# Own keys laid down twice, and one matmul over 120 rows for their high and low values, in a cross attention and mixture of experts kernel

## What is computed

```python
x = x + xattn(layernorm(x), ctx, Wq, Wk, Wv, Wo)   # x: 32 x 56 x 512, ctx: 32 x 1500 x 512
x = x + ffn(layernorm(x), W_gate, b_gate, W_e, b_e)

def xattn(latents, context, Wq, Wk, Wv, Wo):       # 16 heads of 96, 4 key heads
    hidden = concatenate([context, latents], axis=1)        # 1500 + 56 rows
    q, k, v = latents @ Wq.T, hidden @ Wk.T, hidden @ Wv.T
    attn = softmax(einsum('bkgqd,bksd->bkgqs', q, k) * 96 ** -0.5)
    return einsum('bkgqs,bksd->bkgqd', attn, v) ... @ Wo.T

def ffn(x, W_gate, b_gate, W_e, b_e):              # 8 experts, the best 2 of each row
    top_idx = top_k(x @ W_gate + b_gate, 2)
    y = relu(x @ W_e[e] + b_e[e]) for the two experts
    return mean of the two
```

## Time and profile before

| | |
|---|---|
| time, median of 3 runs | 3424.66 us (3420.46 to 3425.6) |
| time of the profiled execution | 3425.12 us |
| its span in the profile | 3423.4 us |
| mean granted TensorE clock | 0.985 |
| PE busy | 3324.6 us, 97% of the span, 21514 matmuls |
| PEld busy | 3095.0 us, 90% |
| DVE busy | 2038.8 us, 60% |
| ACT busy | 1645.3 us, 48% |
| POOL busy | 1025.0 us, 30% |

### The profile page before, as it was taken

How to read it: one execution, slowest core, us unless ns; L and a number is a source line. 1 busy time by engine, 2 the same in 40 slices (tenths; PEclk the granted TensorE clock), 3 DMA queues, 4 the chain that set the end, 5 groups by cost and what they waited for, 6 DMA issues and landing times. The chain is left out here.

```text
span 3423.4 us, 64146 instructions
## 1 busy us (share of the span) xinstructions
PE 3324.6 (97%) x21514; PEld 3095.0 (90%) x21514; DVE 2038.8 (60%) x3003; ACT 1645.3 (48%) x3145; POOL 1025.0 (30%) x838
## 2 busy tenths in 40 slices
PE   8999999999999999999999999999999999989785
PEld 8989999999999999999999999999999999988674
DVE  5346666666666666666666666666666666665444
ACT  3225555555555555555555555555555555542231
POOL 0042222333323333333333222222222233345252
PEclk9999999999999999999999999999999999999887
DMA  6542222222222212222222222222222222217466
GB/s 222 200 142 62 59 60 64 64 64 64 60 62 62 56 51 61 58 60 63 64 63 64 64 64 64 64 60 63 59 58 63 64 64 64 65 56 209 110 197 209
DMA packets 308535, 284.53 MB, mean 83 GB/s; under 512 B 200826, under 2 KB 257650, under 8 KB 308489
## 3 DMA queue, kind: packets, MB, share of 16 engines
q1 hardware_dynamic: 301961, 265.56, 26.8%
q0 software_dynamic: 6528, 18.39, 1.6%
HBM read 208.31 MB, written 75.54 MB: 83 GB/s over the span
## 5 line engine op out<-in xcount | busy, mean ns | idle before, releaser
L815 PE MATMUL ps_proj<-wv_hi,parts 128*125 128x384 f32 x3072 | 875.6, 339 | 0.0
L760 DVE TENSOR_TENSOR probs_lo<-probs,probs_hi 125x448 fp32r<-125x448 f32 (+1 forms) x896 | 680.6, 776 | 275.7 <-ACT probs_hi L687 263.3
L802 PE MATMUL ps_proj<-parts,wk_hi 128*128 128x500 f32 x2304 | 709.8, 389 | 2.9 <-DVEq L715 2.9
L815 PEld LDWEIGHTS ps_proj<-wv_hi,parts 128*125 128x125 f32 x3072 | 559.9, 185 | 5.8
L143 POOL TENSOR_SCALAR parts<-raw 128x1000 fp32r<-128x1000 f32 (+1 forms) x198 | 239.5, 1210 | 958.1 <-PE ps_proj L815 776.7
L679 ACT ACTIVATE probs<-ps_scores 125x448 f32<-125x448 f32 (+1 forms) x896 | 462.9, 517 | 121.2 <-PE ps_scores L863 78.3
L815 PE MATMUL ps_proj<-wv_lo,parts 128*125 128x384 f32 x1536 | 518.4, 338 | 0.0
L802 PEld LDWEIGHTS ps_proj<-parts,wk_hi 128*128 128x128 f32 x2304 | 430.6, 188 | 91.0 <-DVEq L715 3.2
L687 ACT CAST probs_hi<-probs 125x448 fp32r<-125x448 f32 (+1 forms) x896 | 484.1, 540 | 28.3
L666 ACT CAST values_hi<-ps_proj 125x384 fp32r<-125x384 f32 x384 | 184.4, 480 | 645.4 <-PE ps_proj L815 645.4
L729 DVE TENSOR_TENSOR values_lo<-ps_proj,values_hi 125x384 fp32r<-125x384 f32 x384 | 214.1, 558 | 431.8 <-ACT values_hi L666 429.1
(11 more groups left out here) (199 smaller groups left out, 5720.9 us busy)
## 6 DMA issues: line engine op xcount, KB each, us to landing
raw<-in_ctx SPq DMA_DIRECT2D x192, 500.0 KB, 3.6
qk_hi<-proj_out_hi SPq DMA_DIRECT2D x60, 224.0 KB, 2.0
qk_lo<-proj_out_lo SPq DMA_DIRECT2D x60, 224.0 KB, 2.3
queries_hi<-qk_hi SPq DMA_DIRECT2D x32, 336.0 KB, 3.5
queries_lo<-qk_lo SPq DMA_DIRECT2D x32, 336.0 KB, 3.6
att_raw<-attended SPq DMA_DIRECT2D x128, 84.0 KB
probs<-att_raw SPq DMA_DIRECT2D x31, 336.0 KB, 5.8
probs<-inverse_sums SPq DMA_DIRECT2D x31, 336.0 KB, 3.1
```

Of the source, the lines that this page charges most:

```text
L760: dve.tensor_tensor(prs[1][0:R, u % PRING, 0:N], pr[0:R, u % PRING, 0:N], f(prs[0][0:R, u % PRING, 0:N]), ALU.subtract).then_inc(p_lo, 1)
L802: mm = pe.matmul(pproj[n % 2][:, 0:CS], w["wk"][a][:, j // 3, i * P:(i + 1) * P], ct[v][:, c, j // 3, :], start=(j == 0), stop=(j == 3 * K ...
L815: mm = pe.matmul(pproj[n % 2][0:VT, 0:KD], ct[a][:, t // VTC, j // 3, s], w["wv"][v][:, j // 3, :], start=(j == 0), stop=(j == 3 * KT - 1))
```

## The change

The own keys are laid down twice in the key tiles, at column S and again at column S + 64 (`PAIR`); the eight columns between are zero. The tail's scores are made for 120 columns (`TAIL`) in place of 56, so that rows 0 to 55 and rows 64 to 119 of the scores, the exponentials and the probabilities are the same. The tail's value tile holds the high values in rows 0 to 55 and the low values in rows 64 to 119, with the column of ones only beside the high ones. So the first weighing matmul of the tail gives high and low values with the high probabilities in one, and line 882's matmul is left out for the tail; the third now also adds the low values with the low probabilities. The low values' tile for the own rows is gone, with its fill; two fills of the eight columns are new.

The diff, cut to its core:

```diff
+PAIR = 64
+TAIL = PAIR + Q
...
-        kt = [sb("keys_hi", [HD, KV, SL], F32R), sb("keys_lo", [HD + HALVES, KV, SL], F32R)]
+        kt = [sb("keys_hi", [HD, KV, S + TAIL], F32R), sb("keys_lo", [HD + HALVES, KV, S + TAIL], F32R)]
...
-        vt_lo = sb("values_lo", [VT, NVT + 1, KV, HD], F32R)
+        vt_lo = sb("values_lo", [VT, NVT, KV, HD], F32R)
...
                         rows = k_d[i][b]
-                        sp.dma_start(f(kt[i][0:HD, 0:KTILES, S:SL]),
-                                     rows[:, 0:HD].rearrange("i r q -> r i q")).then_inc(qk_loaded, 16)
-                        for j in range(KTILES):
-                            sp.dma_start(f(kt[i][j * PIECE:(j + 1) * PIECE, KTILES, S:SL]),
-                                         rows[j, HD:P]).then_inc(qk_loaded, 16)
+                        for s in (S, S + PAIR):
+                            sp.dma_start(f(kt[i][0:HD, 0:KTILES, s:s + Q]),
+                                         rows[:, 0:HD].rearrange("i r q -> r i q")).then_inc(qk_loaded, 16)
+                            for j in range(KTILES):
+                                sp.dma_start(f(kt[i][j * PIECE:(j + 1) * PIECE, KTILES, s:s + Q]),
+                                             rows[j, HD:P]).then_inc(qk_loaded, 16)
 
                 def load_v(b):
-                    for i, dst in enumerate((vt_hi[0:Q, NVT, :, 0:HD], vt_lo[0:Q, NVT])):
+                    for i, dst in enumerate((vt_hi[0:Q, NVT, :, 0:HD], vt_hi[PAIR:TAIL, NVT, :, 0:HD])):
...
-                sp.wait_ge(consts, 3)
+                sp.wait_ge(consts, 4)
...
-                for n, ap in enumerate((f(vt_hi[:, NVT]), f(vt_lo[:, NVT]), mrow[:], ident[:], own[:])):
+                for n, ap in enumerate((f(vt_hi[:, NVT]), f(kt[0][:, :, SL:S + PAIR]), mrow[:], ident[:], own[:])):
...
-                for n, (ap, value) in enumerate(((kt[1][HD:HD + HALVES], -1.0), (vt_hi[:, 0:NVT, :, HD:HD + 1], 1.0),
-                                                 (vt_hi[0:Q, NVT, :, HD:HD + 1], 1.0))):
+                for n, (ap, value) in enumerate(((kt[1][HD:HD + HALVES], -1.0), (kt[1][:, :, SL:S + PAIR], 0.0),
+                                                 (vt_hi[:, 0:NVT, :, HD:HD + 1], 1.0), (vt_hi[0:Q, NVT, :, HD:HD + 1], 1.0))):
...
-                    R, N = (VT, 2 * GQ) if j < UNITS - 1 else (Q, GQ)
+                    R, N = (VT, 2 * GQ) if j < UNITS - 1 else (TAIL, GQ)
...
-                        pe.wait_ge(qk_loaded, b * 160 + 160)
+                        pe.wait_ge(qk_loaded, b * 288 + 288)
...
-                        s = slice(t * VT, min((t + 1) * VT, SL))
+                        s = slice(t * VT, t * VT + (VT if t < NVT else TAIL))
...
-                        pe.matmul(pav[0:HD, h % 2, 0:GQ], vt_lo[:, t, h], hi, start=False, stop=False)
+                        if t < NVT:
+                            pe.matmul(pav[0:HD, h % 2, 0:GQ], vt_lo[:, t, h], hi, start=False, stop=False)
```

More of the change, by code:

```diff
@@ L620, in _ @@
                                    pattern=[[-1, HALF]], channel_multiplier=1).then_inc(consts, 1)
-                pool.wait_ge(consts, 4)
+                pool.wait_ge(consts, 5)
                 pool.affine_select(out=own[:], in_=own[:], compare_op=ALU.not_equal, fill=1.0, base=0,
@@ L742, in row_max @@
                 def row_max(b):
-                    dve.wait_ge(consts, 5)
+                    dve.wait_ge(consts, 6)
                     dve.wait_ge(max_done, START + b * PARTS + PARTS)
```

## The result

The changed kernel is slower: 3540.57 us in the median of 6 runs (3538.12 to 3565.24) against 3421.7 us in the median of 6 for the kernel before; the ratio is 1.0366, with a 95% interval of 1.0332 to 1.0400. Predicted were 3513 us, in a range of 3455 to 3560. The profiled execution took 3539.81 us, its span is 3538.0 us: 114.6 us more than before.

A forecast was written before the change was run, and what follows sets the result against it. The prediction took TensorE, busy throughout the attending stage, as the bound. It added 94 us of border stalls and 2 us at the start, less 8 us of matmuls: +88 us on 3425.12, giving 3513 us, range 3455 to 3560.

The forecast's parts named there:

- SP's shift: In SP's queue in every batch: eight more key loads delay what stands behind them by 4.4 us (2.8 to 4.6).
- The landing of the sums: Load of the previous batch's row sums: lands 5.7 us after its issue in the median (4.8 to 6.5).
- The stall: PE at the seventh key tile: new wait of 3.1 us at 29 borders and 2.2 us at two, 94 us.
- The links SP, sums, DVE, PSUM buffer: At batch borders: SP issues the sums late, DVE inverts late, the fifth tile leaves its PSUM buffer late, PE waits.
- the slack: Before PE's seventh key tile: 0.87 us free, less 0.1 us because PE is now earlier.
- The start: Start of the attending stage: the last key load lands 2 us after PE wants it, once.
- The clock: PE's clock halves in the border stalls, 3.4 us per fall; at all 31 borders 3618 us; most borders 8%.
- The matmuls: PE's weighing: 128 low-value matmuls removed, 13.3 us, of which 8 us are gained after deductions (7 to 13).
- two deductions: From the 13.3 us: 3.3 us lost at each batch's first head waiting for DVE, 2 us for wider score matmuls.
- the first (no stall): Rival at the sums' landing: SP's shift under about 0.8 us, no PE stall, only the gain left, 3417 us; 8%.
- the fourth: Rival: removed matmuls' time returns at DVE in every head and SP's shift is absorbed, 3425 us; 3%.
- the third, a smaller stall: Rival at the borders: SP needs 2.8 us for the eight loads, stall 1.5 us, 3463 us in all; 14%.

The follow-up runs named there:

- e1: Changed kernel with the second copies' eight key loads issued on SP behind the load of the row sums, with their own semaphore: 3430.03 us, ratio 1.0026.
- e3: Changed kernel with SP's order untouched, but DVE inverts the row sums three key tiles later: 3428.93 us, ratio 1.0023.
- e8: Changed kernel without the low keys' second copy (zero columns), so four extra loads per batch in place of eight: 3458.94 us, ratio 1.0099.
- e2b: Changed kernel's loads and data layout, but the tail done over 56 rows with line 882's matmul back, as before the change: 3537.43 us, ratio 1.0331.
- e5: Changed kernel without the second copies' loads, and with DVE's low split of the tail over 56 rows, not 120: 3419.43 us, ratio 0.9986.
- e4: Changed kernel without the second copies' loads, their columns filled with zeros once: 3427.53 us, ratio 1.0020.
- e7: Changed kernel with second copies loaded behind the load of the row sums and the tail's low split over 56 rows: 3419.52 us, ratio 0.9985.
- e6: Kernel before the change with DVE's low split of the tail on 120 rows in place of 56: 3432.84 us, ratio 1.0025.

## Why the prediction was right, point by point

**Range, direction and cause were right**; the time was 28 us too low, 27 in the profiled execution. In the order of its steps:

- *SP's shift*, put at 4.4 us with bounds of 2.8 and 4.6: 4.14 us. A second copy is issued somewhat faster than a first, and 0.33 us of the shift are the own low values' load, which the prediction had at nothing. (The lower bound took 0.35 us for the shortest issue of the earlier trace rows; 0.33 and 0.34 stand there too.)
- *The landing of the sums*, 5.7 us after the issue: 5.7 again (4.7 to 6.5).
- *The stall*, 3.1 us at 31 borders, 94 us: 2.77 us and 85.8 us in the matmuls' starts, 2.93 us and 90.9 us by the weight loads' waits. The links SP, sums, DVE, PSUM buffer are each confirmed, the first by e1, the third by e3, the slack by e8.
- *The start*, 2 us: not there in the profiled execution, but by chance. The clock fell at that place and made PE late enough; in e2b, where it stayed up, a wait came there and cost 0.8 us.
- *The clock* was a rival for most borders and left out of the sum. It fell in 15 of 31, and the cost of a fall was put at 3.4 us from the one seen in the trace before; it is 1.5 us in twelve of them and 2.8 in three, since most falls here last half as long and the loss at half clock is a little under half. **This term, 26.6 us, is the largest of the miss.**
- *The matmuls*, put at a gain of 8 us (7 to 13): **this step failed.** Its two deductions were right in kind: in e5 the first head gives nothing, and two heads give their 0.10 us each. But the last head gives nothing either, as what it gains is lost again where PE begins the loop anew: from a batch's last weighing matmul to the second key matmul of the next it takes 0.47 us in e5 and 0.36 in the kernel before (means of 29 turns); why was not tried. And the sentence "Exp, high and low split of that unit keep their 224 elements per partition and only use more partitions: nothing" is the one that fell. The duration stayed but for 0.008 us; the turn between DVE and POOL did not, and that costs 0.4 us in each batch. By the timed ratio of e4 the part cost 7 us in place of giving 8. By the batches of the profiled executions it cost 5.9 us, so 14 us of the miss.
- *The miss as a whole*, 114.7 us in place of 88 between the profiled executions: the clock 26.6 and the matmuls 13.9 one way, the smaller stall 8.2, the start 2 and the 3.6 us outside the loop the other way, 26.7 in all. So the time came within 27 us partly by luck: the errors add up to 40 us one way and 14 the other.
- *The rivals*: the first (no stall) and the fourth fell with e2b; the third, a smaller stall, did not come. e8 made one, at a shift of 2.2 us. By the prediction's own slack that gives a stall of 3.1 - 2.2 = 0.9 us, and a batch of e8 takes 0.95 us more than one of e4 (means of 29). That its time, 3459 us, lies beside the third rival's 3463 is luck: the rival has a stall of 1.5 us and a gain of 8 us by the matmuls, where e8 has 0.9 us and a loss. The dispatch of about 50 ns, which the Trainium skill (DMA: Bandwidth & Descriptors, section "Anatomy of one DMA — SWDGE (gpsimd) path") gives for GpSimd's path, does not describe SP's here: the second copies' issues take 0.37 to 0.45 us each.

The signs that were named came: 1536 matmuls at the former line 882, sums 14.8 us behind the query load, DVE's wait at 144.6 us for 160 foretold, a batch every 92.9 us on average for 92.

## What to carry to other kernels

Adding DMAs to a queue is priced not by their bytes and not by who waits for them, but by what stands behind them in the queue, and by the in-order engine that waits for that; if a slack of 0.9 us is all there is, eight issues of 0.4 us are too many, and putting them (or the waiting instruction) somewhere else makes them cost next to nothing (e1 and e3 stand 2.5 and 1.4 us above e4, e7 0.1 above e5). A short stall of TensorE may cost a third as much again through the clock (26.6 us on 85.8 here), by chance from pass to pass. And where VectorE and GpSimd work from SBUF at once, an instruction whose own time stays the same to a hundredth of a microsecond can still change which of them goes first.

## What had not been expected of the hardware

- The length of PE's idle time alone does not tell whether the clock falls. At the start of the stage, after 2.85 to 2.87 us of idle PE, it fell in the profiles of the changed kernel and of e3, e4, e5, e6 and e8 and stayed up in those of the kernel before, e1 and e2b. At the borders of the changed kernel it stayed up after 3.02 us and fell after 3.07 us, but it also fell after 1.78 us (PE's idle time up to 496.41). In e8, with at most 1.64 us at a border, it never did.
- Two runs of the changed kernel stood at 3562.59 and 3565.24 us, some 25 us above the other four, with a mean clock of 0.973 in place of 0.978. By these means the clock stood at half for some 37 us longer; at the price of the falls above (26.6 us for 61) that is an estimated 16 us. The rest is open, since only one execution of the kernel was profiled.
- The load of 84 KB of own low values takes SP 0.82 us to issue into the high tile and 0.49 us into the low one, where a row's heads lie without a gap.
- An operation on 120 partitions in place of 56, with the same elements per partition, turned the order of two engines in all 32 batches; by itself it ends less than a hundredth of a microsecond later.
